# Half of the load DMAs of an attention and FFN kernel are issued by ScalarE's queue in place of GpSimd's

## The reference, cut to what matters

```python
x = L0_attn_hidden_states                      # 4 x 2048 x 4096, float32
xn = _layernorm(x)
# attention: 32 heads of 128, causal, ALiBi bias
qkv = xn @ w_attn + b_attn                     # 4096 -> 12288
attn = softmax(mask(q @ k.T * (1/128) + slopes * rel))
a = (attn @ v) @ w_proj + b_proj               # 4096 -> 4096
# gated FFN
hits = softmax(xn @ centroids.T / 0.1) > 0.01  # 64 clusters
query_sel = any(hits, axis=1); cluster_sel = any(hits, axis=0)   # over all 8192 tokens
f = where(query_sel[:, None] & cluster_sel[assignments][None, :], xn @ weight.T + bias, 0)
return x + a + f
```

## Time and profile before

| | us |
|---|---|
| median of the timed runs (2) | 7306.1 (7282.47 to 7329.73) |
| the profiled execution | 7132.11 |
| its span on the slowest core | 7130.6 |
| spans of the eight cores | 7054.1 to 7130.6 |
| PE busy | 4619.5 |
| DVE, ACT, POOL busy | 1804.2, 1447.6, 1531.1 |

### The profile page before, as it was taken

The page is one execution under the profiler, slowest core; times in us unless marked ns, Lnnn a source line. Parts: engine busy times, 40 slices in busy tenths (PEclk is TensorE's granted clock), DMA queues, the critical chain, the costliest instruction groups (busy, mean ns, idle before and its releaser), DMA issues.

```text
span 7130.6 us, 80009 instructions; the slowest of 8 cores (7054.1 to 7130.6 us)
## 1 busy us (share of the span) xinstructions
PE 4619.5 (65%) x20715; PEld 1965.4 (28%) x20715; DVE 1804.2 (25%) x4169; ACT 1447.6 (20%) x2628; POOL 1531.1 (21%) x2644
## 2 busy tenths in 40 slices
PE   2218898898889884555455555535555556787786
PEld 1103343333333331111111111112222222333333
DVE  4421111111111112232323232235533331222222
ACT  4320000000000001122221212113344441222222
POOL 0112222222222222323333232300000002222222
PEclk9999999999999996666665667656655558888888
DMA  4322222222222224333333333321111115444444
GB/s 130 118 83 83 79 78 80 82 76 82 81 76 83 79 76 145 112 100 114 103 114 104 110 112 103 114 81 47 47 41 43 45 38 158 152 144 129 149 136 127
DMA packets 379099, 687.07 MB, mean 96 GB/s; under 512 B 60129, under 2 KB 227041, under 8 KB 378657
## 3 DMA queue, kind: packets, MB, share of 16 engines
q1 hardware_dynamic: 266866, 346.56, 16.1%
q0 software_dynamic: 111792, 335.40, 15.1%
HBM read 606.22 MB, written 75.50 MB: 96 GB/s over the span
## 4 chain that ended last, share of the span: by engine, by line
PE 50%; DMA 16%; DVE 12%; issue 8%; ACT 7%; POOL 4%; SPq 1%; DVEq 1%; ACTq 0%; POOLq 0%
PE p2p L87 25%; DMA d3x<-xT_all 9%; PE qp L87 7%; PE f5b L87 6%; PE f5a L87 6%; ACT a4e L80 4%; POOL d3q L80 3%; DMA p2w<-w_attn 3%; DVE statc L80 2%; PE a4po L87 2%; PE a4pt L87 2%; DVE d3r L80 1%; DVE p2o L80 1%; DVE a4o L80 1%; ACT p1n L80 1%
## 5 line engine op out<-in xcount | busy, mean ns | idle before, releaser
L87 PE MATMUL p2p<-xn_fm,p2b 128*128 128x512 bf16 x8192 | 1891.1, 395 | 233.8 <-DVE p2b L80 140.0
L87 PEld LDWEIGHTS p2p<-xn_fm,p2b 128*128 128x128 bf16 x8192 | 821.5, 101 | 1303.2 <-issue 411.4
L87 PE MATMUL f5a<-ofm,f5pb 128*128 128x512 bf16 x2048 | 551.5, 394 | 237.1 <-DVE f5pb L80 237.1
L87 PE MATMUL d3pd<-d3b,centbf 128*64 128x512 bf16 x512 | 309.7, 605 | 586.0 <-ACT d3q L80 306.9
L87 PE MATMUL qp<-xno,qb 128*128 128x512 bf16 x2048 | 478.8, 399 | 176.8 <-DVE qb L80 176.8
L87 PE MATMUL f5b<-xno,f5fb 128*128 128x512 bf16 x2048 | 541.7, 388 | 54.0 <-DVE f5fb L80 54.0
L80 DVE CAST d3b<-d3x 128x512 bf16<-128x512 f32 x512 | 324.8, 634 | 870.0 <-DMA d3x<-xT_all 825.0
L80 DVE CAST p2b<-p2w 128x256 bf16<-128x256 f32 x512 | 157.1, 307 | 1481.3 <-PE p2p L87 1436.1
L87 PE MATMUL a4po<-a4a,a4e 128*128 128x129 bf16 x2304 | 332.5, 270 | 294.4 <-ACT a4e L80 280.4
L80 ACT ACTIVATE p2o<-p2p,battn 128x512 bf16<-128x512 f32 x128 | 88.1, 688 | 2050.3 <-PE p2p L87 2041.1
L80 POOL CAST p2b<-p2w 128x256 bf16<-128x256 f32 x512 | 208.7, 408 | 1281.2 <-DMA p2w<-w_attn 1073.5
(11 more groups left out here) (115 smaller groups left out, 4039.4 us busy)
## 6 DMA issues: line engine op xcount, KB each, us to landing
d3x<-xT_all SPq DMA_DIRECT2D x257, 256.0 KB, 4.2
p2w<-w_attn SPq DMA_DIRECT2D x512, 128.0 KB, 2.2
p2w<-w_attn POOLq DMA_DIRECT2D x512, 128.0 KB, 2.5
f5f<-ffn_wT POOLq DMA_DIRECT2D x512, 128.0 KB, 3.0
f5p<-w_proj SPq DMA_DIRECT2D x512, 128.0 KB, 2.8
d3x<-xT_all POOLq DMA_DIRECT2D x255, 256.0 KB, 3.1
qw<-w_attn POOLq DMA_DIRECT2D x256, 128.0 KB, 2.8
qw<-w_attn SPq DMA_DIRECT2D x256, 128.0 KB, 2.8
```

The lines of the kernel that those rows point to most:

```text
L87: return getattr(self.e, method)(*args, **kw)
```

## The change

Four groups of load DMAs that POOL issued are now issued by ACT, at the same place in the written program and with the same waits: the second half of each x tile in the normalising stage (48 DMAs, two for each of 24 tiles), the odd weight slots of K and V (512) and of Q (256), slots 3 to 5 of the routing part (255), and all f5f loads of the output stage (512). Stores stay on POOL, SP's loads and all casts stay where they were. Six new semaphores aq20 to aq25 count the weight loads.

```diff
+        aq2 = [Ch(es, nc, f"aq2{i}") for i in range(6)]
...
-                    PO.dma(posq[6 + s], xt[s][:, 2048:3072], src[:, 2048:3072],
+                    AC.dma(acq[s], xt[s][:, 2048:3072], src[:, 2048:3072],
                            waits=wts)
-                    PO.dma(posq[6 + s], xt[s][:, 3072:4096], src[:, 3072:4096])
+                    AC.dma(acq[s], xt[s][:, 3072:4096], src[:, 3072:4096])
...
                         qeng, qch = ((SY, wsq[s]) if s % 2 == 0
-                                     else (PO, posq[s]))
+                                     else (AC, aq2[s]))
...
                                 qeng, qch = ((SY, wsq[s]) if s % 2 == 0
-                                             else (PO, posq[s]))
+                                             else (AC, aq2[s]))
...
                                 xqe, xch = ((SY, dsq[s]) if s < 3
-                                            else (PO, acq[s - 3]))
+                                            else (AC, acq[s - 3]))
...
-                            PO.dma(posq[s], wft[s][:],
+                            AC.dma(aq2[s], wft[s][:],
                                    ffn_wT[kc * 128:(kc + 1) * 128,
                                           fp_ * 256:(fp_ + 1) * 256],
                                    waits=[wf_done[s]])
```

More of the change, by code:

```diff
@@ L257, in emit_all @@
                     SY.dma(sq[1 + s], xt[s][:, 1024:2048], src[:, 1024:2048])
-                    PO.dma(posq[6 + s], xt[s][:, 2048:3072], src[:, 2048:3072],
+                    AC.dma(acq[s], xt[s][:, 2048:3072], src[:, 2048:3072],
                            waits=wts)
-                    PO.dma(posq[6 + s], xt[s][:, 3072:4096], src[:, 3072:4096])
+                    AC.dma(acq[s], xt[s][:, 3072:4096], src[:, 3072:4096])
                     fills = [(sq[1 + s], sq[1 + s].n),
-                             (posq[6 + s], posq[6 + s].n)]
+                             (acq[s], acq[s].n)]
                     xd_dv[s] = DV.op("reduce_sum", statc[:, 0:1], xt[s][:],
@@ L1019, in emit_all @@
                                 wfb[s][:], wft[s][:],
-                                waits=[(posq[s], posq[s].n),
+                                waits=[(aq2[s], aq2[s].n),
                                        (PE.ch, fb_done[s])]))
```

## The result

The changed kernel is faster, by more than twice what was forecast. Its median is 6913.7 us (11 runs, 6713.1 to 7081.5); the kernel before, run on the same chips in turn with it, had 7285.6 (10 runs). The ratio is 0.947 with a 95% interval of 0.944 to 0.949. (Between the two medians lie 372 us.) The profiled execution took 6731.25 us against 7132.11 before, 401 us less; the forecast had 176 less. Runs of this program spread by a few per cent with the clock that a die is granted, so the ratio is that of the runs in which neither die had less than its usual clock, and all that follows compares such executions, in parts rather than totals wherever a total mixes causes.

A forecast was written before the change was run, and what follows sets the result against it. No engine was taken as full; stages wait, largely for loads standing right ahead of their consumer in an engine's in-order stream. Terms -7 - 138 + 260 - 328 + 37 = -176 took 7306 to 7130 us, range 6920 to 7420.

The forecast's parts named there:

- x_full: Normalising, x_full tiles: ACT's half tile issued only after normalising, so the sum starts later, +3 us x 16 = +48.
- Part Q: Q weight loads: ACT's chain of load, landing, cast takes 2.9 us a pair against PE's 1.88, +260 us.
- Output: Output groups: ACT's f5f loads and casts take 4.1 us a pair against PE's 3.46, +37 us.
- x_own: Normalising, own tiles: load no longer behind POOL's stores, DVE's 8 us wait goes, about -7 x 8 = -55 us.
- K and V: K and V groups: second wait of 2.9 us and 1.4 us of low clock go, x 32 = -138 us.
- Routing: Routing part: six steps take 8.45 us against 12.1 to 12.6, -20.5 us a round, -328 us.
- 3L + 5.2: Routing: loop time for two turns, L being a load's landing, taken as 3.9 us; gives 8.45 us a turn.
- 3, landings at their floor: Rival, chance 0.12: L 2.1 in Q, 3.1 in routing, PE-bound output, K and V -180; -452, 6854 us.
- 1: Rival, chance 0.15: in-line landings on ACT 0.6 us longer in Q, output and routing; +375, 7505 us, slower.
- 2: Rival, chance 0.18: routing gains little, landings stretch and the turn stays at 11.3 us; +243, 7373 us.
- 4, that only the issuer changes: Rival, chance 0.12: waits move one for one from POOL to ACT and nothing nets; 7306 us.

The follow-up runs named there:

- experiments 3: Changed kernel with only part Q's odd weight loads back on POOL: 6573.9 us, Q part 29.9 us.
- experiments 4: Changed kernel with only routing's slots 3 to 5 back on POOL: 7246.5 us, routing part 64.6 to 65.6 us.
- experiment 5: Changed kernel with only K and V's odd weight loads back on POOL: 6871.95 us, a group 61.9 us.
- Experiment 2: Changed kernel with ACT's x-tile loads also waiting for ACT's previous instruction, the normalising: 6833.41 us, an x_full tile 18.3 us.
- Experiment 1: Changed kernel with ACT's odd loads of part Q also waiting for the cast ahead of them: 6861.96 us, Q part 47.6 us.
- Experiment 6: Changed kernel with ACT's f5f loads in output also waiting for ACT's previous instruction: 6947.65 us, a group 85.4 us.
- Experiment 11: Changed kernel with ACT issuing routing's load 5 ahead of its square 4: 6658.7 us, routing part 39.4 to 40.8 us.
- experiment 7: Changed kernel with ACT's loads of Q and routing moved to SP: profiled execution 6306.4 us, routing part 30.4 us.
- experiment 9: Changed kernel with part Q's odd loads still on ACT but two odd slots ahead of their own cast: 6584.1 us, Q part 29.9 us.

## Why the prediction was wrong in size and right in direction

**The reading of what bounds each stage held.** The waits named for K and V and for routing are those that went, the new ones in Q are those that came, and each part undone alone gave its own part back (experiments 3, 4, 5).

**The step that failed** is what stands ahead of ACT's issue. In normalising the forecast says "ACT issues half of tile t+1 only after normalising tile t", and in Q it takes "cast and waits" from "POOL's same cycle, 3.10 less its landing 2.5": 0.6. Output and the routing loop are added up in the same way. But ACT's DMA starts 0.02 us after the start of the instruction ahead of it. Taking POOL's cycle over to ACT was the mistake: on POOL cast and issue come one behind the other, on ACT the issue runs beside the arithmetic. With the 0.6 replaced by what is measured:

- *x_full*, +48 forecast, 0 measured. Experiment 2, with the assumed order, costs 30 us in these tiles. The assumption also hid the second effect, halves that travel apart and land in half the time.
- *Part Q*, +260 forecast (46 us), +170 measured (40.6). Experiment 1, with the order assumed, gives 47.6, or 113 us more. The landing of 2.3 was close (2.16 median, 2.37 mean); what is added to it in a pair is 2.54 less 2.37, some 0.2 and not 0.6.
- *Output*, +37 forecast, -9 measured. The pair was 4.1 in the forecast and is 3.53, with the landing as assumed (2.6 by the page). Experiment 6 gives 4.68 and 179 us more with the order assumed: there the forecast's own working would have been 0.6 too low, most of it in the landing (3.10).

In these three terms the forecast was 184 us too high, of the 225 between its -176 and the -401 of the profiled executions. Put in by hand, the order costs 30, 113 and 179 us. In Q and output that is more than enough, since the forecast was too low for its own order; in x_full it is too little for the 48, since the forecast took a landing of 8 us where experiment 2 has 6.9. About 35 of the 225 us are the rest of the table, for which no cause is shown.

**x_own** (-55; -52) and **K and V** (-138; -146) came out. The first is partly luck: with the order that the forecast assumed an own tile takes 27.2 us (experiment 2), which is -39. In the second the idle time inside a group went from 2.93 to 0.17 us as forecast. The time at the low clock (1.2 GHz) went from 9.0 to 3.7 us a group, but 1.9 and 0.2 of it fell into that idle time; half of the rest is lost, which makes 1.8 us, where the forecast gave 1.4.

**Routing** (-328; -328) came out to the microsecond, and that proves less than it seems. The formula 3L + 5.2 took L as 3.9; measured were 3.05 by ACT (two of the three legs) and 3.67 by SP, which by the formula gives 7.5 us a turn. The failed step stands here too: load 5 goes out beside square 4 and not behind it, which makes it 7.2 (core 5):

```profile
2680.92 0.63 ACT L80 ACTIVATE d3q<-d3x 128x512 bf16<-128x512 f32 x1 [3.90 <-DMA d3x<-xT_all]
2681.05 0.33 ACTq L99 DMA_DIRECT2D d3x<-xT_all  x1
```

Seen was 8.4. Too long a landing made up for something that the loop leaves out. Experiment 11 shows that load 5's place is a part of the loop only. The mechanism (loads behind squares) is shown by experiments 4 and 7; the exact size was luck.

**The rivals.** 3, landings at their floor (6854), came nearest, though for another reason: its Q and routing terms did not occur, the output term was -9 rather than -40. 1 and 2 asked for landings 0.6 us longer or an ACT issue as slow as POOL's (0.33 measured), and for landings that stretch with the rate; d3x landed in 3.1 us by ACT as it had by POOL, and in 3.7 by SP after 4.2. 4, that only the issuer changes, is excluded by the 401 us. The Trainium skill's rule beside it ("DMA: Bandwidth & Descriptors", section "Issuing engines are not separate DMA queues") says that another issuer saves only the sequencer's time to start the DMA. The traces agree as far as the issuer alone goes: d3x lands in 3.1 us by ACT and by POOL, p2w in 2.2 by ACT and in 2.5 by POOL (core 7 after and in experiment 5), of which 0.2 may be the shorter issue. What the change won and lost beyond that came from the place in the stream, of which the rule doesn't speak: moving 256 issues of the same 128 KB within ACT's own stream (experiment 9) is worth 10.7 us a part. The Trainium skill's rule on descriptor writing ("SBUF — State Buffer", section "SBUF: two separate sides") would show as landings by POOL that are longer in DVE's company; no run isolates this, and d3x by POOL, beside DVE's casts, stays at 3.1 us.

**The range.** Its ends vary the landings and PE's low clock, each with the same assumed order; the doubt about the order itself was in none of them. The change of -372 between the medians lies between the forecast's -176 and rival 3's -452, and the range's low end stopped 66 us short of that rival's time.

## What to carry to other kernels

A load belongs on an engine and at a place where nothing ahead of it in the stream waits for the data of its neighbours: here an otherwise idle SP queue for all loads gave 0.881 of the time before, and where a busy engine must issue, moving the load two slots ahead of its own consumer gave back the whole loss. For a load behind a compute instruction on ACT, count from that instruction's start unless the load is made to wait for it. Before taking a cycle time from one engine over to another, split it into what overlaps and what doesn't.

## What the hardware showed that was not expected

- ACT starts a DMA 0.01 to 0.07 us after the start of the ACT instruction ahead of it, in routing mostly 0.13, with casts of 0.40 and with a normalising of 3.80 us (2624.91 and 2624.93; 165.43 and 165.45; 5702.83 and 5702.90). Made to wait for that instruction, it starts 0.48 us after the start of a cast. POOL's load in K and V started 0.48 us after the start of its 0.40 us cast without being made to wait (1015.73 and 1016.21). ACT's issue takes 0.33 us for a weight load and up to 0.45 for 512 KB, POOL's took about 0.52.
- Halves of x tiles (1 MB, two DMAs), issued by two queues 3.9 us apart rather than together, land in 4.3 and 4.5 us instead of 8.8 and 6.8, or 6.9 and 7.1 in experiment 2.
- Routing's 256 KB loads on one queue instead of two: a part of 30.4 us rather than 44.9, with landings of 4.0 rather than 3.1 and 3.7, and 262 GB/s on this core in the row of experiment 7.
